# Attention batch kernel: value products of two steps behind one another, with task and step tables of their own

## The reference, cut to what matters

```python
xn = _layernorm(x)
qkv = xn @ W_attn + b_attn                  # split in q, k, v; 16 heads of 16; rope on q, k
att = softmax(mask(q @ k.T / 4))            # causal, 1024 x 1024 per head and batch
s = (att @ v) @ W_proj + b_proj
g = silu((silu(xn @ wg.T) * (xn @ wu.T)) @ wd.T)
out = x + s * g
```

## Time and profile before

| | |
|---|---|
| median of three runs | 1334.45 us |
| the profiled execution | 1334.66 us |
| its span in the trace | 1332.8 us |
| TensorE busy | 1278.7 us (96%) |
| VectorE busy | 986.3 us (74%) |
| ScalarE busy | 948.3 us (71%) |
| GpSimd busy | 687.3 us (52%) |
| the chain that ended last | 90% of it on TensorE |

### The profile page before, as it was taken

How to read it: one execution, slowest core, us unless ns; L and a number is a source line. 1 busy time by engine, 2 the same in 40 slices (tenths; PEclk the granted TensorE clock), 3 DMA queues, 4 the chain that set the end, 5 groups by cost and what they waited for, 6 DMA issues and landing times.

```text
span 1332.8 us, 30434 instructions
## 1 busy us (share of the span) xinstructions
PE 1278.7 (96%) x11399; PEld 572.6 (43%) x11399; DVE 986.3 (74%) x1930; ACT 948.3 (71%) x2090; POOL 687.3 (52%) x850
## 2 busy tenths in 40 slices
PE   2899999999999999999999999999999999999996
PEld 1334433445344443544444453444435454444433
DVE  6788787877877877787777778778777878767721
ACT  2147777786777777777777867777777777778673
POOL 4116443584437734475545844377344755455642
PEclk9679999999999999999999999999999999999988
DMA  2630022302041020400213020410204002120001
GB/s 84 182 81 2 20 62 63 99 1 71 27 128 34 9 89 18 128 18 23 76 57 105 1 73 26 127 34 4 94 17 128 18 17 82 54 75 2 23 11 48
DMA packets 56854, 73.70 MB, mean 55 GB/s; under 512 B 9026, under 2 KB 35074, under 8 KB 56708
## 3 DMA queue, kind: packets, MB, share of 16 engines
q1 hardware_dynamic: 56420, 71.38, 17.8%
q10 hardware_dynamic: 288, 0.39, 0.1%
HBM read 46.01 MB, written 25.17 MB: 53 GB/s over the span
## 4 chain that ended last, share of the span: by engine, by line
PE 90%; DVE 4%; ACT 3%; DMA 1%; POOL 1%; issue 1%; ACTq 0%; POOLq 0%; SPq 0%; DVEq 0%
PE ring L741 30%; PE acc L733 22%; PE st L679 16%; PE ring L703 8%; PE ring L828 4%; PE ring L714 3%; PE ring L803 3%; DVE mx_a L1036 2%; ACT pexp L908 2%; PE ring L837 1%; PE ring L818 1%; PE ring L751 1%; DVE mx_b L1036 1%; DMA xn<-in_x 1%; DMA k_st<-parts_scratch 0%
## 5 line engine op out<-in xcount | busy, mean ns | idle before, releaser
L908 ACT ACTIVATE pexp<-st 128x512 f32<-128x512 f32 (+3 forms) x1536 | 659.0, 490 | 108.7 <-PE st L679 101.9
L1036 DVE TENSOR_REDUCE mx_a<-ring 128x1 f32<-128x512 f32 (+3 forms) x896 | 529.6, 646 | 76.0 <-PE ring L714 42.5
L1256 POOL TENSOR_SCALAR_AFFINE_SELECT pexp<-pexp 128x512 f32<-128x512 f32 x256 | 163.3, 638 | 541.8 <-ACT pexp L908 541.0
L733 PE MATMUL acc<-pexp,v_pad 128*17 128x512 f32 (+3 forms) x3072 | 324.7, 495 | 5.1 <-POOL pexp L1256 4.2
L679 PE MATMUL st<-q_st,k_st 50*128 50x512 f16 (+3 forms) x1536 | 282.5, 334 | 8.8 <-ACT pexp L908 8.3
L703 PE MATMUL ring<-k_st,q_st 48*128 48x512 f16 (+3 forms) x1536 | 264.2, 332 | 8.0 <-DMA k_st<-parts_scratch 5.0
L1036 DVE TENSOR_REDUCE mx_b<-ring 128x1 f32<-128x384 f32 (+3 forms) x384 | 212.2, 595 | 66.0 <-PE ring L714 65.7
L679 PEld LDWEIGHTS st<-q_st,k_st 50*128 50x128 f16 x1536 | 82.9, 93 | 375.2 <-ACT pexp L908 276.4
L1287 POOL TENSOR_TENSOR hf<-ga,ups 128x512 f32<-128x512 f32 x96 | 122.1, 1272 | 14.6 <-issue 10.4
L714 PE MATMUL ring<-tri,ident 64*128 64x128 bf16 (+2 forms) x1536 | 121.9, 219 | 0.0
L1296 POOL TENSOR_TENSOR hT<-hf,hT 128x512 f16<-128x512 f32 x96 | 111.3, 1160 | 3.8
(11 more groups left out here) (113 smaller groups left out, 1521.2 us busy)
## 6 DMA issues: line engine op xcount, KB each, us to landing
parts_scratch<-parts SPq DMA_DIRECT2D x32, 512.0 KB, 2.8
q_st<-parts_scratch SPq DMA_DIRECT2D x192, 64.0 KB, 2.2
k_st<-parts_scratch SPq DMA_DIRECT2D x186, 64.0 KB, 2.2
xn<-in_x SPq DMA_DIRECT2D x8, 1024.0 KB, 5.9
xo<-in_x SPq DMA_DIRECT2D x32, 256.0 KB, 2.8
out<-xo SPq DMA_DIRECT2D x32, 256.0 KB, 2.2
q_st<-mT SPq DMA_DIRECT2D x128, 4.0 KB
pexp<-in_w_attn SPq DMA_DIRECT2D x1, 768.0 KB, 4.7
```

The costliest lines, as they stand in the source:

```text
L733: mm = nc.tensor.matmul(acc[32 * j:32 * j + D + 1, CH - w:CH], v_pad[:, kb, GH * g + j, :], pexp[:, GH * (n % NSET) + j, 0:w], start=n in ...
L908: nc.scalar.activation(pexp[:, GH * (n % NSET) + j, 0:w], st[:, (GH * n + j) % NST, 0:w], ACT.Exp, scale=1.0 / (QK_SCALE * np.sqrt(D))).th ...
L1036: nc.vector.reduce_max(dst, ring[:, b, 0:len(heads) * w].rearrange("p (s w) -> p s w", w=w), AX.X)\
L1256: nc.gpsimd.affine_select(out=t, in_=t, compare_op=ALU.is_ge, fill=0.0, base=0, pattern=[[0, GH], [1, P]], channel_multiplier=-1).then_inc ...
```

## The change

Three things are changed together.

1. TensorE no longer makes the value products of the step before at the end of every slot. At the end of an even slot it makes those of the two steps before, one behind the other, and at the end of an odd slot none.
2. The order of the blocks in a group is another. The widths of steps 0 to 11 were 512, 384, 256, 128, 512, 512, 512, 512, 512, 384, 256, 128 and are 512, 128, 384, 256, 512, 512, 512, 256, 512, 384, 512, 128. Diagonal steps are now 0 to 3, 7, 8, 9 and 11. `DIAG_ORDER` and `FULL` are permuted, so that steps 0, 3, 6 and 10 have no maxima in the second half.
3. The tables of tasks are other ones. The same tasks stand in fewer slots: 45 of the 48 slots of a middle batch had work of TensorE in their first half, now 32 have (38 and 31 in the first batch, 42 and 34 in the last). Slots without are now 2, 3, 8, 11, 14, 15, 19, 24, 26, 27, 31, 35, 38, 39, 44 and 47; they were 16, 36 and 40.

Beside these, the task UPU on GpSimd waits for `h_low` and not `h_high`, and the mask at the very end stands under `if is_diag(STEPS - 1)`, which is true.

```diff
-BLOCKS = [(0, 0), (0, 1), (0, 2), (0, 3), (1, 0), (1, 1), (1, 2), (1, 3), (1, 4), (1, 5), (1, 6), (1, 7)]
-DIAG_ORDER = (0, 1, 2, 3, 4, 5, 6, 7, 8, 9, 10, 11)
+BLOCKS = [(0, 0), (0, 3), (0, 1), (0, 2), (1, 0), (1, 1), (1, 2), (1, 6), (1, 4), (1, 5), (1, 3), (1, 7)]
+DIAG_ORDER = (1, 3, 5, 11, 4, 9, 10, 0, 7, 8, 2, 6)
...
-FULL = (0, 2, 3, 4, 6, 7, 8, 9)
+FULL = (1, 2, 4, 5, 7, 8, 9, 11)
...
 TASKS = {
-    0: [("DN", 1, 2)],
-    1: [("UPG", 0, 0), ("FT", 0)],
...
+    0: [("UPG", 0, 0), ("DN", 1, 2), ("FT", 0), ("FT", 1)],
+    1: [("DN", 1, 3), ("FP", 0)],
+    2: [("XC", 0), ("XC", 1)],
...
-                        elif slot > 0:
-                            values(i, *divmod(slot - 1, STEPS))
-                        elif kind != "first":
-                            values(i - 1, GROUPS - 1, STEPS - 1)
+                        elif slot % 2 == 0 and (slot > 0 or kind != "first"):
+
+                            for back in (2, 1):
+                                at = slot - back
+                                values(i if at >= 0 else i - 1, *divmod(at % SLOTS, STEPS))
 
             def epilogue():
-                values(B - 1, GROUPS - 1, STEPS - 1)
+                for n in (STEPS - 2, STEPS - 1):
+                    values(B - 1, GROUPS - 1, n)
...
-                    wait(pool, h_high, k - 2)
+                    wait(pool, h_low, k - 2)
```

More of the change, by code:

```diff
@@ L63 @@
 TASKS = {
-    0: [("DN", 1, 2)],
-    1: [("UPG", 0, 0), ("FT", 0)],
[L66 to L84, removed]
[6 rows of a table removed]
[L91 to L109, removed]
+    0: [("UPG", 0, 0), ("DN", 1, 2), ("FT", 0), ("FT", 1)],
+    1: [("DN", 1, 3), ("FP", 0)],
+    2: [("XC", 0), ("XC", 1)],
+    4: [("UPU", 0, 0), ("LNS", 0), ("LNS", 1), ("FP", 1)],
+    5: [("V", 1, 1), ("V", 0, 1), ("LNS", 2), ("LNS", 3)],
@@ new lines @@
+    6: [("UPG", 0, 1), ("UPG", 0, 2), ("LNR",)],
+    7: [("UPU", 0, 1), ("YT", 3, 1)],
+    8: [("LNA", 6)],
+    9: [("UPU", 0, 2), ("MT", 1), ("YT", 0, 0)],
+    10: [("LNA", 4), ("UPG", 0, 3)],
+    12: [("UPG", 0, 4), ("LNA", 2)],
+    13: [("UPU", 0, 3)],
+    14: [("LNA", 7)],
+    16: [("UPG", 0, 5), ("V", 1, 0), ("FT", 3), ("LNA", 1)],
+    17: [("LNA", 5), ("UPU", 0, 4), ("UPU", 0, 5)],
+    18: [("YT", 1, 0), ("FT", 2)],
+    20: [("TX", 1, 1), ("LNA", 3)],
+    21: [("MT", 2), ("YT", 0, 1), ("LNA", 0)],
@@ new lines @@
+    22: [("TX", 0, 1), ("FP", 2)],
+    23: [("TX", 0, 0), ("TX", 1, 0), ("QK", 0, 0, 1), ("DN", 0, 0)],
+    25: [("QK", 0, 1, 1), ("QK", 0, 0, 0), ("QK", 0, 1, 0), ("DN", 0, 1)],
+    28: [("DN", 0, 2)],
+    29: [("QK", 1, 0, 1), ("DN", 0, 3)],
+    30: [("UPG", 1, 0), ("UPG", 1, 1), ("UPU", 1, 0), ("UPU", 1, 1)],
+    32: [("UPG", 1, 2), ("QK", 1, 1, 0), ("UPU", 1, 2)],
+    33: [("MT", 3), ("YT", 1, 1)],
+    34: [("V", 0, 0)],
+    36: [("UPG", 1, 3), ("FP", 3)],
+    37: [("UPU", 1, 3), ("YT", 2, 0)],
@@ L110 @@
+    40: [("QK", 1, 1, 1), ("UPG", 1, 4)],
+    41: [("UPG", 1, 5), ("UPU", 1, 4), ("UPU", 1, 5)],
+    42: [("QK", 1, 0, 0)],
+    43: [("YT", 3, 0)],
+    45: [("DN", 1, 0), ("MT", 0), ("YT", 2, 1)],
+    46: [("DN", 1, 1)],
 }
@@ L121 @@
 END_TASKS = {
[L122 to L134, removed]
+    28: [("DN", 0, 2)],
+    29: [("DN", 0, 3)],
+    30: [("UPG", 1, 0), ("UPU", 1, 0)],
+    31: [("UPG", 1, 1), ("UPU", 1, 1)],
+    32: [("UPG", 1, 2), ("UPU", 1, 2)],
+    33: [("MT", 3), ("YT", 1, 1), ("UPG", 1, 3)],
+    34: [("UPU", 1, 3), ("UPG", 1, 4)],
+    35: [("UPU", 1, 4)],
+    36: [("FP", 3)],
+    37: [("YT", 2, 0), ("UPG", 1, 5)],
+    38: [("UPU", 1, 5)],
+    42: [("YT", 3, 0), ("DN", 1, 0)],
+    43: [("FT", 0, "end"), ("FT", 1, "end"), ("DN", 1, 1)],
     44: [("FP", 0, "end")],
-    45: [("FP", 1, "end")],
+    45: [("YT", 2, 1), ("FP", 1, "end")],
+    46: [("DN", 1, 2, "end")],
+    47: [("DN", 1, 3, "end")],
 }
@@ L1380, in epilogue @@
             def epilogue():
-                mask(B - 1, GROUPS - 1, STEPS - 1)
+                if is_diag(STEPS - 1):
+                    mask(B - 1, GROUPS - 1, STEPS - 1)
             run(pool, body, prologue, epilogue)
```

## The result

The changed kernel takes 1361.1 us (median of four runs, 1360.8 to 1361.5) where the kernel before, with a fourth run, takes 1333.8: a ratio of 1.021, with an interval of 1.0192 to 1.0228. It is slower, as forecast, but by 27 us and not by 65.

A forecast was written before the change was run, and what follows sets the result against it. TensorE, busy for 96% of the span, was taken to bound the kernel. 1334.7 - 55.8 (changeovers) - 15.2 (old waits) + 122 + 6.4 (new waits) + 7 (GpSimd) gave 1399 us, 4.8% slower; range 1355 to 1442.

The forecast's parts named there:

- One sign that I had named: In a middle batch, TensorE idle some 18 us for under 1 before, nearly all put down to L908's exponentials.
- The old waits: Score waits for exponentials in slots 16, 36 and 40, without TensorE tasks, would go: 1.9 us a batch, -15.2 us.
- The changeovers: Fewer switches of TensorE's array mode at 0.098 us each: value products -37.6 us, task slots -18.2, together -55.8 us.
- the junction: Where an even slot's two value sets meet on the same strips: put at nothing, at worst 0.10 us, 19 us in all.
- the tasks' 18.2 us: Changeovers around TensorE tasks: 93 fewer task slots, two changeovers of 0.098 us each, saving 18.2 us.
- GpSimd, +7 us: FP's products, copies and masks queue on GpSimd from slot 2, delaying step 3's value products: +0.9 us a batch, +7 us.
- 2.7, 1.1 and 3.1: TensorE's time in us for slot 2, slot 3, and slot 4 up to its value products.
- The new waits, 122 + 6.4 us: Scores waiting for exponentials: 15.2 us a batch around odd slots (+122), 0.8 in even slots without tasks (+6.4).
- The covered waits: Rival: ScalarE runs ahead, only some 10 us of new waits stand against the savings: 1274 us; chance 0.10.
- The point that I named for that rival: Break-even: a mean new wait of 0.35 us in 24 odd slots and 0.8 elsewhere, 71 us in all.
- a third of my waits: Variant of the covered-waits rival with a third of the forecast new waits: 1311 us.
- The falling clock: Rival: TensorE's clock halves for some 7 us around slots 2 to 4; once a batch 1421 us, twice 1444; chance 0.13.

The follow-up runs named there:

- the run with the maxima between: Changed kernel, but in even slots the second half's maxima stand between the two value sets instead of ahead of both: 1384.2 us, 1.0375.
- more cover: Changed kernel, but in even slots with a TensorE task the first half's maxima are issued ahead of its two scores: 1350.8 us, 1.0130.
- less cover: Changed kernel, but in the second half of odd slots the maxima are issued ahead of the two scores: 1371.9 us, 1.0289.
- the run with the pairs alone: Kernel before, with its block order and task tables, but value products made in pairs at the end of even slots: 1424.0 us, 1.0676.
- the tables alone: Changed kernel's block order and task tables, but value products of one step at the end of every slot, as before: 1438.1 us, 1.0784.
- the values late: New tables and block order, unpaired value sets two steps behind their scores, copies of the accumulated result one slot later: 1371.8 us, 1.0291.
- four score banks: Changed kernel with four score banks and three banks in the ring: 1475.9 us, 1.1060.
- the copies later: Changed kernel, but ScalarE's copies of the tasks UPU, V and FP come one half slot later, behind the exponentials: 1431.9 us, 1.0738.

## Why the prediction was right and wrong

**The direction and its mechanism were right.** The chain score, exponential, third next score takes 1.14 us for 512, and with a copy ahead 1.25. The rows of after have 1.24 and 0.93 for my 1.25 and 0.93. Step by step the waits measured in a middle batch (mine in brackets): behind step 1 0.64 twice, 0.42, 0.31 (0.66, 0.51, 0.39); step 5 0.80 three times and 0.63 (0.82, 0.71); step 7 0.42 twice (0.50) and, without a task, 0.63 (0.67); step 9 0.57 (0.60). Step 3 loses 0.63 over its two places (0.67), step 11 0.56 three times and 0.65 (0.57, 0.73). The sum is 15.8 us where I had 15.2 + 0.8. One sign that I had named did not come: the profile's busy time shows TensorE idle for 4.5 us a batch and not 18, since it hides these waits.

**The size was wrong: +27 us and not +65.** The steps of the sum that were mis-sized, over the whole program:

- *The old waits, 15.2 us.* They were 34 us. I took only the three slots without a task of a middle batch. The narrow value sets of 128 did not cover the chain either (0.19 us behind each in five places a batch, and 0.10 behind the three), and the first and the last batch, which have more slots without tasks or maxima, waited 7.3 and 7.9 us where I had put 1.9. This is the largest error, 19 us.
- *The changeovers, 2 x 0.098 an island of value products.* An island costs 0.27 (the run with the maxima between), so 192 of them saved 51 and not 38 us: 14 us. I had put the junction at nothing, the low end, and the truth lay below my low end: I reasoned that it could hardly be better, while the earlier trace rows held the stagger beside the changeover. That is 0.04 us of the 0.07 by which an island was mis-sized; the rest is the difference of the run to the rows, and open. For the tasks' 18.2 us I have no other number.
- *GpSimd, +7 us.* Nothing. TensorE's second wait in line is not there, as the rows of slot 2 to 4 show:

```profile
407.45 0.64 POOL L1249 TENSOR_SCALAR_AFFINE_SELECT pexp<-pexp 128x512 f32<-128x512 f32 x1
...
407.52 0.52 PE L724 MATMUL acc<-pexp,v_pad 128*17 128x384 f32 x4
```

The mask of step 3 is done at 408.09, 8.5 us after slot 2 begins at 399.56, as I had it (8.6). But TensorE comes to the value products of step 2 only at 407.52, 1.1 us later than the 6.9 that my 2.7, 1.1 and 3.1 make. One task ahead of them, FP, keeps it for 1.9 us, and I had given it half. Those of step 3 start at 408.18, 0.09 us behind the mask: nearly a wait.
- *The new waits, 122 + 6.4 us.* They were 134, 6 us more, for the first and the last batch waited 16.8 and 22.4 us.

With the measured terms the sum nearly closes: -51 - 18 - 34 + 134 = +31, for 27.3 in the medians and 26.2 in the spans (with 0.24 for an island +36).

**The rivals.** The covered waits are refuted: more cover and less cover moved the time the way of the latency, and no wait of it shrank by itself. The point that I named for that rival, 71 us of new waits, was too low: the measured savings are 51 + 18 + 34 = 103 us, so the change would have paid with new waits under 103. It has 134, 3.9 us a batch too many. Two numbers of that rival were rounded loosely: a third of my waits gives 1307 us by my terms and not 1311, and 71 us in all is a mean of 0.34. The falling clock is refuted for this kernel: it stayed full through its middle batches, as it did in the run with the pairs alone, whose waits are longer. It fell in the middle batches of four experiments (the tables alone, the values late, four score banks, the copies later).

**What stays open.** How the waits for ring banks add up where maxima or copies move was in each case read afterwards, not foretold; the first batch grew by 0.4 us only, and its terms were not taken apart. In the last batch of the kernel before the clock stood at half for 6.8 us (from 1280.9; the earlier trace rows show a part); the changed kernel has no such stretch there. That would be a gain of at most 3.4 us that the sum leaves out. No run takes the block order and the task tables apart, or `h_low` and `h_high`.

## What to carry to other kernels

Before work is put together to save changeovers, ask what it stood between: here a value set was worth 0.24 to 0.27 us as an island and 0.2 to 1.1 us as cover for a chain of 0.9 to 1.25 us from score to exponential to the buffer's next use. Pairing pays only where other work covers that chain; undoing a third of the pairs, behind wide steps, took most of the loss away. When a change removes waits as well as adding them, sum the old ones over the whole program from start times, edges included, and not over the few that a view names; an engine's busy share doesn't show them where two matmuls run side by side.

## What the runs showed of the hardware

Two sets of four column products behind one another cost less than their columns and starts apart: the stagger of the second set's starts lies under the first set's stream (297.27 after 296.84, 0.43 us for a pass of 0.427). And the clock: with a wait of 0.2 to 0.8 us behind every odd slot, TensorE kept the full clock through all middle batches of the changed kernel, and so it did with 0.4 to 1.1 us in the run with the pairs alone. In the run with the tables alone it fell 0.6 us into a stand of 2.06 us, and 6.8 us at 1.2 GHz followed, though TensorE was at work again after 1.4 of them.
